# TensorE takes over the sums of the two wide graph aggregations, products are written back into the ring

## The reference

```python
Wh = (x @ W.T).reshape(N, H, C)                  # N = 6250 nodes
e = e_left[src] + e_right[dst]                   # 206250 edges, self loops among them
e = jnp.where(e >= 0, e, NEG_SLOPE * e)
e_max = segment_max(e, dst, num_segments=N)
e_exp = jnp.exp(e - e_max[dst])
denom = segment_sum(e_exp, dst, num_segments=N)
alpha = e_exp / (denom[dst] + EPS)
out = segment_sum(Wh[src] * alpha[:, :, None], dst, num_segments=N)
```

## Time and profile before

| | us |
|---|---|
| median of three runs | 10115.43 |
| span of the profiled execution | 10110.4 |
| first wide aggregation, first gather to last result | 1012 to 3676 |
| ranking, narrow aggregation with 4 experts, ranking | 3676 to 6399 |
| second wide aggregation | 6399 to 8751 |
| last dense layer, 8 experts, output | 8751 to 10110 |
| DVE busy | 5594.3 (55%) |
| POOL busy | 5337.1 (53%) |
| PE busy | 2288.8 (23%) |

### The profile page before, as it was taken

The page is one execution under the profiler, slowest core; times in us unless marked ns, Lnnn a source line. Parts: engine busy times, 40 slices in busy tenths (PEclk is TensorE's granted clock), DMA queues, the critical chain, the costliest instruction groups (busy, mean ns, idle before and its releaser), DMA issues. The chain is left out here.

```text
span 10110.4 us, 54577 instructions
## 1 busy us (share of the span) xinstructions
PE 2288.8 (23%) x9111; PEld 1752.0 (17%) x9112; DVE 5594.3 (55%) x8828; ACT 1093.7 (11%) x2533; POOL 5337.1 (53%) x5411
## 2 busy tenths in 40 slices
PE   2112000000000002146555512000000000129995
PEld 1111000000000001135444411000000000116663
DVE  8764588788777677523333275455656556421111
ACT  1101000000000001112222201000000000002221
POOL 0025656666676654455555345776666777542221
PEclk7555555555555555578777755555555555559997
DMA  4051333433333353411111162433333333620004
GB/s 142 22 159 50 97 82 87 122 99 98 101 101 98 102 113 74 122 23 33 29 28 28 30 172 89 109 100 92 101 98 101 106 99 99 129 97 30 30 30 117
DMA packets 458121, 869.43 MB, mean 86 GB/s; under 512 B 175134, under 2 KB 294860, under 8 KB 448192
## 3 DMA queue, kind: packets, MB, share of 16 engines
q0 software_dynamic: 239536, 575.99, 23.0%
q1 hardware_dynamic: 167648, 182.04, 6.2%
q10 hardware_dynamic: 50788, 110.02, 3.3%
HBM read 693.35 MB, written 180.71 MB: 86 GB/s over the span
## 5 line engine op out<-in xcount | busy, mean ns | idle before, releaser
L914 POOL DMA_INDIRECT agg_ring<-table,agg_idx x4320 | 4275.8, 990 | 2329.8 <-issue 1323.4
L1042 DVE TENSOR_TENSOR agg_part<-agg_ring,agg_prob 128x2048 f32 x420 | 964.4, 2296 | 631.8 <-issue 556.2
L1080 DVE TENSOR_TENSOR agg_wide<-agg_wide,agg_part 128x2048 f32<-128x2048 f32 x420 | 960.4, 2287 | 14.4
L1786 PE MATMUL dense_tp<-all_ident,dense_xn 128*128 128x128 f32 x100 | 23.9, 425 | 2570.3 <-issue 2543.7
L1408 PE MATMUL agg_hp<-agg_xt,agg_w 128*128 128x256 f32 x1600 | 446.4, 439 | 579.4 <-ACT agg_ht L1378 340.3
L2208 DVE TENSOR_TENSOR experts_h<-experts_sg,experts_hp 128x682 f32<-128x682 f32 x106 | 91.8, 866 | 779.7 <-ACT experts_sg L2191 779.7
L2158 PE MATMUL experts_hp<-mixture_w,experts_xt 128*128 x1696 | 518.2, 458 | 0.6 <-ACT experts_xt L2187 0.6
L1408 PEld LDWEIGHTS agg_hp<-agg_xt,agg_w 128*128 128x128 f32 x1600 | 352.4, 224 | 663.8 <-ACT agg_ht L1378 360.4
L1786 PEld LDWEIGHTS dense_tp<-all_ident,dense_xn 128*128 128x128 f32 x100 | 20.3, 228 | 2571.9 <-issue 2544.5
L2129 POOL DMA_INDIRECT yc<-experts_ysb,experts_list x105 | 103.7, 987 | 685.2 <-DVE experts_ysb L2217 685.2
L1422 PE MATMUL agg_yp<-agg_w,agg_ht 128*128 128x256 f32 x1600 | 405.3, 411 | 231.0 <-remote 174.5
(11 more groups left out here) (421 smaller groups left out, 6520.8 us busy)
## 6 DMA issues: line engine op xcount, KB each, us to landing
agg_ring<-table,agg_idx POOLq DMA_INDIRECT x4320
y<-agg_ysb ACTq DMA_DIRECT2D x25, 1024.0 KB
rank_y<-y SPq DMA_DIRECT2D x10, 2560.0 KB
rank_x<-x SPq DMA_DIRECT2D x30, 640.0 KB
copies<-first_sort_words SPq DMA_DIRECT2D x16, 1024.0 KB
copies<-last_sort_words ACTq DMA_DIRECT2D x16, 1024.0 KB
x<-rank_x SPq DMA_DIRECT2D x20, 640.0 KB
agg<-agg_res ACTq DMA_DIRECT2D x98, 128.0 KB
```

The source lines that it names most:

```text
L914: pool.indirect_dma_start(out=self.ring[:, to:to + self.RW], out_offset=None, in_=self.table, in_offset=bass.IndirectOffsetOnAxis(ap=index ...
L1042: return dve.tensor_tensor(to[:, :].rearrange("p (j h c) -> p j h c", j=UNIT, h=H), ring[:, ds(st.at(at_u), UNIT * RW)].rearrange("p (j w) ...
L1080: dve.tensor_tensor(wide[:, :], wide[:, :], part[:, :], ALU.add).then_inc(widened, 1)
```

## The change

The sums leave DVE. The product of a unit is written over the unit in the ring; PE then adds the eight slots with eight matmuls of 256 columns against the identity matrix, into one PSUM tile `sums`, over all units of a chunk, and PE gives the unit back to POOL. The shared last unit goes into its own tile `last`, and PE adds it at the end of the chunk. DVE adds `sums` of the chunk before to `acc` when the next chunk has been scored, and at the end of a tile forms `res = acc + sums`, then divides it. The tile `wide`, the adds into it and the three folds are gone.

Waits of DVE and ACT that stood on register instructions now stand on one-element `memset`s or copies, several addresses are computed earlier, and the loop over whole units has no wait. The sizes of a tile are stored as 16-bit numbers, six for each tile instead of five 32-bit ones. In the second wide aggregation the tile loop of DVE and PE becomes a hardware loop; ACT's stays unrolled.

```diff
-        wide, part, summed = s.sb("wide", [P, UC]), s.ps("part", [P, UC]), s.sb("summed", [P, CW])
+        last, sums = s.sb("last", [P, UC]), s.ps("sums", [P, 512])
+        passed = s.sb("passed", [1, 6])
...
+                        if later:
+                            dve.wait_ge(tile_done, t)
+                            dve.memset(passed[:, 0:1], 0.0)
+                        dve.wait_ge(summed, kk)
+                        dve.tensor_tensor(acc[:, :], acc[:, :], sums[:, 0:CW], ALU.add).then_inc(merged, 1)
                         dve.wait_ge(probs, kk)
-                        first = u0 & 1
-                        weigh(u1, nu + first, wide).then_inc(tail, 1)
...
-                        with dve.Fori(n0, n1) as n:
-                            dve.wait_ge(widened, n)
-                            weigh(n, u + first, part).then_inc(taken, 1)
-                            dve.wait_ge(taken, n)
-                            dve.tensor_tensor(wide[:, :], wide[:, :], part[:, :], ALU.add).then_inc(widened, 1)
+                        dve.memset(passed[:, 5:6], 0.0)
+                        weigh(ending, last[:, :].rearrange("p (j h c) -> p j h c", j=UNIT, h=H), in_prob).then_inc(tail, 1)
+                        with dve.Fori(u0, u1) as n:
+                            at = st.at(n)
...
+                            weigh(at, unit, u).then_inc(weighed, 1)
                         dve.tensor_reduce(dsum[:, :], prob[:, 0:SC].rearrange("p (j h) -> p h j", h=H), AX.X, ALU.add).then_inc(totalled, 1)
...
-                        dve.tensor_tensor(wide[:, 0:4 * CW], wide[:, 0:4 * CW], wide[:, 4 * CW:8 * CW], ALU.add).then_inc(quartered, 1)
-                        dve.tensor_tensor(wide[:, 0:2 * CW], wide[:, 0:2 * CW], wide[:, 2 * CW:4 * CW], ALU.add).then_inc(halved, 1)
-                        dve.tensor_tensor(summed[:, :], wide[:, 0:CW], wide[:, CW:2 * CW], ALU.add).then_inc(folded, 1)
-                        dve.tensor_tensor(acc[:, :], acc[:, :], summed[:, :], ALU.add).then_inc(combined, 1)
...
+                    dve.wait_ge(summed, kn + 1)
+                    dve.tensor_tensor(res[:, :], acc[:, :], sums[:, 0:CW], ALU.add).then_inc(parts_done, 1)
+                    dve.tensor_tensor(res3, res3, den[:, :].unsqueeze(2).to_broadcast([P, H, C]), ALU.mult).then_inc(tile_done, 1)
...
+                def add_up(of, wide, opens, closes):
+                    for i in range(UNIT):
+                        mm = pe.matmul(sums[:, 0:CW], S["ident"][:, :], of[:, ds(i * wide, CW)], start=opens and i == 0, stop=closes and i == UNIT - 1)
+                    return mm
...
+                        pe.wait_ge(merged, kk)
+                        pe.wait_ge(weighed, n0)
+                        add_up(unit, RW, True, False).then_inc(taken, 1)
+                        with pe.Fori(n2, n1) as n:
+                            unit = ring[:, ds(st.at(n + (cfg.RU - 1)), UNIT * RW)]
+                            pe.wait_ge(weighed, n)
+                            add_up(unit, RW, False, False).then_inc(taken, 1)
+                        pe.wait_ge(tail, kk)
+                        add_up(last, CW, False, True).then_inc(summed, 1)
```

More of the change, by code:

```diff
@@ L1114, in _ @@
+                if beside.parts:
+                    for t in range(1, NT):
+                        tile(t, True)
+                else:
+                    with dve.Fori(1, NT) as t:
+                        tile(t, True)
             @block.tensor
             def _(pe):
-                for t in range(NT):
-                    beside.tensor(pe, t)
+                def add_up(of, wide, opens, closes):
+                    for i in range(UNIT):
+                        mm = pe.matmul(sums[:, 0:CW], S["ident"][:, :], of[:, ds(i * wide, CW)], start=opens and i == 0, stop=closes and i == UNIT - 1)
+                    return mm
@@ new lines, in tile @@
+                def tile(t):
+                    ng, nk, c0, k0, _ = sizes_of(pe, t)
+                    with pe.Fori(0, nk) as k:
+                        gg = c0 + k * ng
+                        kk = pe.snap(k0 + k + 1)
+                        u0, u1 = gg // UNIT, (gg + ng) // UNIT
+                        n0, n1 = pe.snap(u0 + 1), pe.snap(u1 + 1)
+                        n2 = pe.snap(n0 + 1)
+                        unit = ring[:, ds(st.at(u0), UNIT * RW)]
+                        pe.wait_ge(merged, kk)
[7 more added lines that the diff above has]
+                        add_up(last, CW, False, True).then_inc(summed, 1)
@@ L1119, in _ @@
+                pe.wait_ge(sized, 5)
+                pe.wait_ge(const, 6)
+                if beside.parts:
+                    for t in range(NT):
+                        tile(t)
+                        beside.tensor(pe, t)
+                else:
+                    with pe.Fori(0, NT) as t:
+                        tile(t)
             @block.scalar
@@ new lines, in lay @@
+                    act.activation(er[:, ds(to, H)], ring[:, ds(mine, H)], ACT.Copy).then_inc(laid, 1)
+                    with act.Fori(g0, end) as g:
+                        place = nc.s_assert_within(g - g0 + 1, 1, CH // WIDE + 1, skip_runtime_bounds_check_because="a chunk has up to 64 slots")
+                        act.activation(el[:, ds(place * GH, GH)].rearrange("p (j h) -> p j h", h=H),
+                                       ring[:, ds((g % (cfg.RS // WIDE)) * (WIDE * RW), WIDE * RW)].rearrange("p (j w) -> p j w", w=RW)[:, :, CW:CW + H], ACT.Copy).then_inc(copied, 1)
```

131 lines of the change are left out of this document (68 added, 63 removed).

## The result

The changed kernel took 10386.28 us (median of 4 runs, 10351.93 to 10449.24), the kernel before, beside it, 10120.69 us (4 runs, 10109.69 to 10134.28): ratio 1.0267, 95% interval 1.0232 to 1.0302. Not only did the gain of 470 us not come, 266 us were lost.

What follows compares the result with a forecast made beforehand. DVE's chain was taken as the bound in both wide aggregations, with POOL's gathers just behind. 10110.4 - 350 (first) - 120 (second) = 9640 us for the span, 9645 for the median of the runs; range 9495 to 9950.

Steps and rivals of the forecast that it cites:

- POOL stands right behind DVE, 531 us to be had: Both wide aggregations: POOL's waits for DVE, 384.7 and 146.2 us, are the most that can be given back.
- gathers' spans 2290 and 2210: First and second wide aggregation: us that the gathers would span after the change, with POOL's waits under 80 and 30.
- Folds gone, products 2288 ns, gathers no longer stretched: Both wide aggregations: DVE's products keep 2288 ns; gathers no longer stretched by folds, counted as 25 us in each.
- PE can start 10.0 us after scoring: Tile chain: scoring 4.6 us, exponential 0.8, products of the shared and first units 2.3 each come before PE's sums.
- The sort's 208 records: First aggregation: sort transposes queue behind PE's sums, 10 rounds, each up to 10 us later; 60 us of waits left.
- So a unit is 3.45 us at full clock: PE's sums: a unit's 8 matmuls, 16 records, priced from a warm burst in the earlier trace.
- PE 20.7 us a tile: First aggregation: 5.3 units at 3.45 us plus 2.4; whole tile chain 31.9 us against POOL's 46.0.
- Rival 3: PE's register instructions slow, 11 a unit at 1.4 us: about 11400 us, in both aggregations about 13200; 10%.
- The 699 ns of DVE's register instructions: Second aggregation: median, against 168 in the first; staying slow gives -80 us, otherwise -171; -120 taken, bounds -190 and 0.
- rival 1: Wide aggregations: DVE's instruction stream remains the bound; first -250, second 0 to -60, about 9830 us; 17%.
- rival 2: Wide aggregations: PE stays at half clock, a unit takes 6.9 us; about 9980, up to 10150 us; 10%.
- rival 4: Nothing gained: waits come back through DVE's new wait on `summed`; 10080 to 10150 us; 3%.

Runs made afterwards that it cites:

- e7: Changed kernel with 4 matmuls of 512 columns a unit instead of 8 of 256, on the uncharged chip: 8926.76 us, 0.9795 of the kernel before.
- e4: Changed kernel, but DVE writes products into four buffers of their own and frees the ring itself: 11513.79 us, 1.1392 of the kernel before.
- e13: Changed kernel with 16 matmuls of 128 columns a unit instead of 8 of 256, on a charged chip: 11429.24 us, 1.1278 of the kernel before.
- e9: As e7, but DVE adds each unit's upper four slots on the lower four, PE sums the rest; uncharged chip: 9153.35 us, 1.0043 of the kernel before.
- e17: Changed kernel with a POOL memset of 256 columns after each gather: 10097.25 us, 1.0002 of the kernel before.
- e6: Hand-overs alone, no kernel computed, with other partners and gathers than e5, on the chip where the kernel before takes 9113.67 us: turns of 1.22 to 3.89 us.
- e10: e6 again where the kernel before takes 10124.19 us: turns 22.40 us with 4 matmuls of 512 columns, 3.89 with gathers 1.66 us apart.
- e5: No kernel computed, DVE and a partner hand a value to and fro: with PE's 8 matmuls 3.89 us quiet or beside plain copies, 44.80 beside gathers.

## Why the prediction was wrong

- *POOL stands right behind DVE, 531 us to be had; gathers' spans 2290 and 2210.* Right in kind: where nothing is charged, e7's waits are nearly gone and its first span is 2263. The second sum was wrong: 2334.9 us, and with it the 2189, 44.7 a tile and 2210, leaves out 65 of the 1728 gathers, and the whole stream spans 2416.7. The waits were rightly read, so the forecast didn't hang on it.
- *Folds gone, products 2288 ns, gathers no longer stretched.* Right for the products, 2281 ns. The mean gather falls from 1004 to 948 ns in the second aggregation, but only from 996 to 986 in the first, where the sort still runs beside.
- *PE can start 10.0 us after scoring.* Right: 10.7 us in the first aggregation, 8.8 in the second. PEclk rose to 0.69 in both, as said. The sort's 208 records are 13 rounds and not 10, which decided nothing.
- **The step that failed: "16 records in a warm burst take 3.45 us from start to start [...] So a unit is 3.45 us at full clock", and PE 20.7 us a tile.** PE's records in undisturbed tiles give just that, 18.6 to 20.1 us from first to last start with four units. But records don't say when the work is handed over. I took the price of 32 instructions from a burst in the earlier trace rows, and had no row of PE beside a long stream of gathers. Charged, a unit is 44.8 us and the tile's chain 10.0 + 5.3 x 44.8 = 247, against 46.0 of gathers. It isn't as bad as that in the kernel, because the ring fills, POOL stops and the charge ends some 5.5 us later.
- *Rival 3, PE's register instructions slow.* Nearest to the truth, at 10%. Its sign and place were right; its price (11 instructions a unit, 1.4 us) counted the wrong instructions: all 32 of the engine are charged, not those of the stream. Its 11400 us are near what came when DVE gave the ring back (e4, 11514) and when PE had twice the instructions (e13, 11429), but that is luck: the sum behind it is another.
- *The 699 ns of DVE's register instructions in the second aggregation.* I wrote that I don't know the cause, bounded it by DVE alone (0 to -190 us) and went on. It was the same charge: such instructions are over 0.4 us long in no aggregation of e7 to e9 and e17. The earlier trace rows even had the figure: 7.02 us for a trip with 5 register instructions, 1.4 us each. It was to be read as a warning for any engine that gets many small instructions there. The range (9495 to 9950) had no room for it.
- *Rivals 1, 2 and 4.* DVE's stream wasn't the bound, PE's clock rose, and the new wait on `summed` did swallow the gain, as rival 4 says, but not by the chain that it names.

## What to carry to other kernels

PE's records here didn't tell when its result was there; the waiting engine's row did: where a wait ends by "remote" although the engine named has long been done, time the hand-over by itself before building on it. Unexplained slow register instructions on one engine are a state that others will share; before work moves from few large instructions to many small ones, count them, and price them in the worst state seen. And where waits regulate each other (a full ring stops the gathers, and that ends the charge), moving one wait to another engine can cost more than it gave.

## What the runs showed of the hardware that I had not expected

- The charge: 1.40 us an instruction on PE, DVE and ACT, after 10 to 30 us of gathers 1.36 us apart or less on average; none with 1.44 us or more. There were signs of it on every chip of this study but one. On that one, no register instruction is longer than 0.4 us in the trace of e7, and the narrow aggregation, which the change doesn't touch, has its gathers in 1086 us against 1490.
- What serves one instruction in 1.40 us is open. The page's table of issues gives a lead. In e7, uncharged, and in the changed kernel:

```profile
agg_ring<-table,agg_idx POOLq DMA_INDIRECT x4320, 2.8
```

```profile
agg_ring<-table,agg_idx POOLq DMA_INDIRECT x4320
```

The landing time is missing where there is a charge: too few of the gathers' records are there to tell it. A gather has 16 landing events. Of the same program, the trace of e6 holds all 18432, that of e10 3719; in e10's stretch with gathers 1.66 us apart, which isn't charged, 1308 of 1536 are there. So the charge and the loss of records go together. But e5's plain copies, on a charged chip, kept all 4608 of theirs, so it isn't the number of records alone. The Trainium skill (NOTIFIC — the notification-queue block, section 7.1, Overflow) says that the block which writes the timestamped records holds its producers back when its own pipeline is full, and can throttle an engine so. By that rule the charge would be the price of recording, 1.40 us for an instruction and a gather on chips whose records drain slowly. All runs here, the timed ones too, come with a span and a clock, so none was without records; whether a kernel that isn't recorded is charged at all was not tried, and that is the main rival left open here. If it isn't, the uncharged chip is the one to go by, on which the changed kernel itself was never run.
- PE's increments seem to be held apart from its sums: at 8401.51 and 8401.67 us in the changed kernel two increments come 0.16 us apart, though the passes that make them, the last on the ring and the last on `last`, start 4.63 us apart. I have no explanation for this.
